# Two attention layers in one kernel: the squares of the second layer's norm are summed by full-precision products on quarters of the array, and K and V are computed by tokens

## The reference, cut to what matters

```python
def _rmsnorm(t, w):
    inv = rsqrt(mean(t * t, axis=-1, keepdims=True) + EPS)
    return t * inv * w

q = (x @ Wq.T).reshape(b, s, H, HD).transpose(0, 2, 1, 3)
k = (x @ Wk.T).reshape(b, s, HKV, HD).transpose(0, 2, 1, 3)
v = (x @ Wv.T).reshape(b, s, HKV, HD).transpose(0, 2, 1, 3)
q = _rmsnorm(q, q_norm_w)
k = _rmsnorm(k, k_norm_w)
scores = einsum('bkgqd,bksd->bkgqs', q.reshape(b, HKV, G, s, HD), k) / sqrt(HD)
attn = softmax(scores + where(rel > 0, NEG_INF, slopes * rel))
out = einsum('bkgqs,bksd->bkgqd', attn, v) ... @ Wo.T
```

## Time and profile before

| | us |
|---|---|
| median of 3 runs (1780.08 to 1784.43) | 1782.18 |
| the profiled execution | 1786.09 |
| its span, first to last instruction | 1784.4 |
| TensorE matmuls busy | 1732.1 (97%) |
| VectorE busy | 1306.6 (73%) |
| ScalarE busy | 877.3 (49%) |
| GpSimd busy | 789.8 (44%) |

### The profile page before, as it was taken

How to read it: one execution, slowest core, us unless ns; L and a number is a source line. 1 busy time by engine, 2 the same in 40 slices (tenths; PEclk the granted TensorE clock), 3 DMA queues, 4 the chain that set the end, 5 groups by cost and what they waited for, 6 DMA issues and landing times.

```text
span 1784.4 us, 28744 instructions
## 1 busy us (share of the span) xinstructions
PE 1732.1 (97%) x8864; PEld 1439.3 (81%) x8864; DVE 1306.6 (73%) x2317; ACT 877.3 (49%) x2288; POOL 789.8 (44%) x924
## 2 busy tenths in 40 slices
PE   8999999999999989997999999999999998899999
PEld 7888888888888878876788888888888887678887
DVE  5788888887888886534777777777777777755555
ACT  3656666566556553222444444444444444544543
POOL 5334435362534443344545454545454524254442
PEclk9999999999999999999999999999999999999999
DMA  4112122122222121000111010010000002022211
GB/s 148 36 66 80 61 71 94 46 91 75 65 66 81 48 73 60 1 30 1 36 30 30 29 29 29 29 29 29 29 29 29 24 0 78 18 71 59 59 59 48
DMA packets 47711, 87.77 MB, mean 49 GB/s; under 512 B 6576, under 2 KB 6576, under 8 KB 47536
## 3 DMA queue, kind: packets, MB, share of 16 engines
q1 hardware_dynamic: 47664, 87.19, 15.2%
HBM read 77.73 MB, written 9.44 MB: 49 GB/s over the span
## 4 chain that ended last, share of the span: by engine, by line
PE 56%; DVE 6%; ACT 2%; POOL 2%; issue 1%; POOLq 0%; DVEq 0%; ACTq 0%
PE ring L317 10%; PE ring L318 10%; PE ring L319 10%; PE scores L317 3%; PE scores L319 3%; PE scores L318 3%; PE turned L317 3%; PE turned L318 3%; PE turned L319 3%; PE turned L806 2%; PE scores L720 2%; PE turned L792 1%; PE turned L770 1%; PE turned L799 1%; ACT p L832 1%
## 5 line engine op out<-in xcount | busy, mean ns | idle before, releaser
L317 PE MATMUL ring<-xt_hi,w_lo 128*128 128x512 f32 x768 | 304.7, 397 | 3.9 <-DVE qt_lo L953 1.5
L318 PE MATMUL ring<-xt_lo,w_hi 128*128 128x512 f32 x768 | 303.8, 396 | 0.0
L319 PE MATMUL ring<-xt_hi,w_hi 128*128 128x512 f32 x768 | 303.7, 395 | 0.0
L317 PE MATMUL ring<-wd_hi,ot_lo 128*128 128x512 f32 x512 | 208.3, 407 | 9.4 <-DVE xt_lo L501 4.2
L823 ACT CAST pt_hi<-turned 128x512 fp32r<-128x512 f32 x192 | 100.9, 592 | 222.0 <-PE turned L799 218.8
L318 PE MATMUL ring<-wd_lo,ot_hi 128*128 128x512 f32 x512 | 202.9, 396 | 0.0
L319 PE MATMUL ring<-wd_hi,ot_hi 128*128 128x512 f32 x512 | 202.9, 396 | 0.0
L581 POOL TENSOR_SCALAR sq_hi<-sq 128x512 fp32r<-128x512 f32 x80 | 55.2, 690 | 284.5 <-ACT sq L849 266.1
L317 PEld LDWEIGHTS ring<-xt_hi,w_lo 128*128 128x128 f32 x768 | 145.1, 189 | 36.6 <-DVE qt_lo L953 2.0
L319 PEld LDWEIGHTS ring<-xt_hi,w_hi 128*128 128x128 f32 x768 | 144.8, 189 | 34.7
L318 PEld LDWEIGHTS ring<-xt_lo,w_hi 128*128 128x128 f32 x768 | 145.0, 189 | 31.5
(11 more groups left out here) (246 smaller groups left out, 4409.6 us busy)
## 6 DMA issues: line engine op xcount, KB each, us to landing
w_raw<-w_attn_dram SPq DMA_DIRECT2D x96, 256.0 KB, 2.9
wd_raw<-w_dense_dram SPq DMA_DIRECT2D x64, 256.0 KB, 2.7
code_early<-codes_dram SPq DMA_DIRECT2D x28, 256.0 KB, 2.7
absmax_early<-absmax_dram SPq DMA_DIRECT2D x56, 128.0 KB, 3.0
kept_dram<-deq_early SPq DMA_DIRECT2D x28, 256.0 KB, 2.1
stage<-kept_dram SPq DMA_DIRECT2D x28, 256.0 KB, 2.7
code_late<-codes_dram SPq DMA_DIRECT2D x14, 256.0 KB, 2.7
absmax_late<-absmax_dram SPq DMA_DIRECT2D x28, 128.0 KB, 2.9
```

The source lines that it names most:

```text
L317: nc.tensor.matmul(o, l_lo, r_hi, start=start, stop=False)
L318: nc.tensor.matmul(o, l_hi, r_lo, start=False, stop=False)
L319: return nc.tensor.matmul(o, l_hi, r_hi, start=False, stop=stop)
```

## The change

What it does, all in the second attention except for one wait:
- The K and Q squares are no longer split. `sq` has a place for each of the four heads. One step `q_rms` per half, in slots 2 and 0 between the two `out` tiles, makes four plain 32-bit products with `ones` (128 partitions x 32 columns) as the stationary operand. Head h writes to partitions 32h to 32h+31 of the side bank, so each sum is there 32 times. VectorE copies the whole bank, and `q_rms_turn` transposes full 128x128 blocks and reads one column of 32.
- K and V are computed together with tokens stationary (`kv` steps, two per half): 48 matmuls of 256 columns in place of 24 of 512. Tokens lie on partitions, so V needs no transpose, and ScalarE sums the squares of K with its accumulator. VectorE keeps K in `k_tok`, multiplies it by its root behind the Newton steps, and `k_norm` transposes it; ScalarE writes `kt_f` and `kt_hi` with the norm's weight as scale, VectorE writes `kt_lo`. GpSimd has no part in it.
- The order: slots 1 and 3 compute Q0, Q1, Q2; slots 2 and 0 compute Q3 and the two `kv` steps. The refills go in the order Q0, Q1, Q2, Q3, K, V. The lead-in and the first slot are rearranged, and the last norm's two token tiles are turned one at a time (`norm_tile`), the first on the side bank.
- SyncE waits for the loop of the second attention to end before it loads the first stages of the feed-forward, because `sq` is larger. An empty instruction stands between its wait and a weight load.

```diff
+REFILL = [[K, Q0, Q1, Q2, Q3, V], [Q0, Q1, Q2, Q3, K, V]]
 def slot_steps(b, rms):
-        tiles = [K, Q0, Q1] if b in (1, 3) else [Q2, Q3, V]
+        tiles = [Q0, Q1, Q2] if b in (1, 3) else [Q3]
...
     t = [("tile", x, half, ahead) for x in tiles]
+    t += [("kv", j, half, ahead) for j in range(2)] if rms and tiles == [Q3] else []
...
-    s += [("k_rms", half)] if rms and tiles[0] == K else []
...
-    s += [("v_turn", half)] if tiles[-1] == V else []
+    s += [("v_turn", half)] if tiles[-1] == V else [("q_rms", half)] if rms and tiles == [Q3] else []
     s += [("k_norm", 1 if b == 1 else 0)] if roots else []
-    s += [("w_next", X) for X in (Q0, Q1)] if rms and b == 3 else []
+    s += [("w_next", X) for X in (Q0, Q1, Q2)] if rms and b == 3 else []
...
-        s += [("out", 1), ("q_rms", half, 0 if tiles[0] == K else 1)]
+        s += [("out", 1)]
 def first_slot_steps(rms):
-        s = [("q_rms", 1, 0), ("tile", Q2, 1, 0)] + softmax[0] + [("w_next", K)] + softmax[1] + [("tile", Q3, 1, 0)]
-        s += [("w_next", Q0)] + softmax[2] + [("tile", V, 1, 0), ("normalise", 1), ("q_rms", 1, 1), ("w_next", Q1)]
-        return s + [("v_turn", 1)] + [("w_next", X) for X in (Q2, Q3, V)] + [("transpose",)]
+        s = softmax[0] + [("tile", Q2, 1, 0), ("w_next", Q0)] + softmax[1] + [("tile", Q3, 1, 0), ("w_next", Q1)]
+        s += softmax[2] + [("kv", 0, 1, 0), ("w_next", Q2), ("normalise", 1), ("kv", 1, 1, 0), ("q_rms", 1)]
+        return s + [("w_next", X) for X in (Q3, K, V)] + [("transpose",)]
 def lead_steps(rms):
-        s = [("norm_stats", [3]), ("tile", K, 0, 0), ("norm_root", [3], "dve"), ("norm_write", 3, "dve")]
-        s += [("tile", Q0, 0, 0), ("tile", V, 0, 0), ("k_rms", 0), ("tile", Q1, 0, 0), ("v_turn", 0)]
-        s += [("q_rms", 0, 0), ("tile", Q2, 0, 0), ("tile", Q3, 0, 0), ("norm_turn", 3), ("q_rms", 0, 1)]
-        s += [("q_rms_turn", 0), ("tile", K, 1, 0), ("roots", 0), ("tile", Q0, 1, 0), ("k_rms", 1)]
-        return s + [("tile", Q1, 1, 0), ("k_norm", 0)]
+        s = [("norm_stats", [3]), ("tile", Q0, 0, 0), ("norm_root", [3], "dve"), ("norm_write", 3, "dve")]
+        s += [("tile", Q1, 0, 0), ("tile", Q2, 0, 0), ("kv", 0, 0, 0), ("tile", Q3, 0, 0), ("norm_tile", 6, True)]
+        s += [("kv", 1, 0, 0), ("q_rms", 0), ("norm_tile", 7, False), ("q_rms_turn", 0), ("roots", 0)]
+        return s + [("tile", Q0, 1, 0), ("k_norm", 0), ("tile", Q1, 1, 0)]
# TensorE
+                    elif step[0] == "kv":
+                        _, j, half, ahead = step
+                        tile = pe_ring_bank(pe).rearrange("p (t d) -> p t d", t=2)
...
+                        for t in range(2):
+                            at = slice(half * HALF + (2 * j + t) * P, half * HALF + (2 * j + t + 1) * P)
+                            for c in range(DC):
+                                ins = mm3(tile[:, t, :], xt_hi[:, c, at], xt_lo[:, c, at], w_hi[:, K:V + 1:V - K, c, :],
+                                          w_lo[:, K:V + 1:V - K, c, :], start=c == 0, stop=c == DC - 1)
...
-                    elif step[0] == "q_rms":
-                        _, half, pair = step
...
-                        for j in range(2):
-                            h = 2 * pair + j
-                            part = (half + 1 + h) % 2
-                            row = pick[:, P - h:2 * P - h]
-                            nc.tensor.matmul(tile, row, sq_lo[:, part, :], start=j == 0, stop=False)
-                            ins = nc.tensor.matmul(tile, row, sq_hi[:, part, :], start=False, stop=j == 1)
+                    elif step[0] == "q_rms":
+                        tile = pe_ring_bank(pe, side=True)
+                        pe_sq.up(HEADS)
+                        pe.wait_ge(s_sq, pe_sq.value())
+                        for h in range(HEADS):
+                            ins = nc.tensor.matmul(tile[32 * h:32 * h + 32, :], ones[:, :], sq[:, h, :], start=True,
+                                                   stop=True)
                         pe_ring_done(ins)
# q_rms_turn, k_norm
-                            ins = nc.tensor.transpose(tile[:, q * ROWS:(q + 1) * ROWS],
-                                                      sumsq[0:ROWS, half, q * P:(q + 1) * P],
-                                                      ident[0:ROWS, 0:ROWS])
+                            ins = nc.tensor.transpose(tile[:, q * P:(q + 1) * P],
+                                                      sumsq[:, half, q * P:(q + 1) * P], ident[:, :])
-                            ins = nc.tensor.matmul(tile[:, q * P:(q + 1) * P],
-                                                   root[:, step[1], q, HEADS:ROWS].to_broadcast([P, P]),
-                                                   ident[:, :], start=True, stop=True)
+                            ins = nc.tensor.transpose(tile[:, q * P:(q + 1) * P], k_tok[:, q, :], ident[:, :])
# ScalarE
+                        for t in range(2):
+                            nc.scalar.activation(k_square[:, t, :], tile[:, t, 0, :], ACT.Square,
+                                                 accum_out=k_sum[:, 2 * j + t:2 * j + t + 1])
...
+                        act_ring_hi(nc.scalar.copy(v_hi[:, at, :], tile[:, :, 1, :]))
# VectorE, behind the Newton steps
+                        nc.vector.tensor_tensor(k_tok[:, :, :], k_tok[:, :, :],
+                                                root[:, half, :, HEADS:ROWS].to_broadcast([P, HALF // P, HD]),
+                                                ALU.mult).then_inc(s_k_scaled, 1)
# GpSimd, k_norm and the squares: gone
-                            split_steps(pool, sq_hi[:, part, :], sq_lo[:, part, :], sq[:, :], s_sq_split)
-                        split_steps(pool, kt_hi[:, cols], kt_lo[:, cols], keys, s_k_ready)
# SyncE
             if not (isinstance(sp_w.turns, int) and sp_w.n < 3):
                 sp.wait_ge(s_w, sp_w.value() - 2)
+                hold(sp)
...
+                eng.wait_ge(s_ring_full, last_slots[1])
                 for k in range(4):
                     load_stage(0, k)
```

More of the change, by code:

```diff
@@ L457, in pool_norm, with pe_norm_turn @@
                                         ALU.add).then_inc(s_shift, 1)
[L458 to L464, removed]
+            elif step[0] in ("norm_turn", "norm_tile"):
+                pool_ring.up(len(turned_tiles(step)))
+        def pe_norm_turn(pe, step):
+            for t, side in turned_tiles(step):
+                b = t // 2
+                tile = pe_ring_bank(pe, side)
                 if xn_last[0] is not None and b == BATCH - 1:
@@ L611, in attention @@
                 ffn_in["xn_last"] = p1[:, :, :].rearrange("p h k -> p (h k)").rearrange("p (t d) -> p t d", d=D)
[L612 to L615, removed]
+                k_tok = sb("k_tok", [P, HALF // P, HD], F32, scope)
+                k_sum = sb("k_sum", [P, HALF // P], F32, scope)
+                k_square = sb("k_square", [P, 2, HD], F32, scope)
                 sumsq = xn
@@ L684, in dve_lead, with pe_weights @@
                                                 as_f32(xt_hi[:, :, at]), ALU.subtract).then_inc(s_lead_lo, 1)
+            def pe_weights(pe, X, g, ahead, b):
+                if rms and b is None:
+                    pe.wait_ge(s_w, WT * (GROUPS + 1))
+                else:
+                    pe.wait_ge(s_w, WT * (GROUPS * layer + g + ahead) + REFILL[layer].index(X) + 1)
             def pe_steps(pe, steps, g, b):
@@ L959, in dve_steps @@
                             ALU.subtract))
-                    elif step[0] == "k_rms":
-                        tile = dve_ring_tile(dve, side=True)
-                        dve_ring_free(nc.vector.tensor_copy(sumsq[0:ROWS, step[1], :], tile[0:ROWS, :]))
+                    elif step[0] == "kv":
+                        _, j, half, ahead = step
+                        tile = dve_ring_tile(dve, after_hi=True).rearrange("p (t x d) -> p t x d", t=2, x=2)
+                        at = slice(2 * j, 2 * j + 2)
+                        nc.vector.tensor_scalar(ms[:, at, HEADS], k_sum[:, at], 1.0 / HD, RMS_EPS, ALU.mult, ALU.add)
+                        nc.vector.tensor_copy(k_tok[:, at, :], tile[:, :, 0, :])
+                        at = slice(4 * half + 2 * j, 4 * half + 2 * j + 2)
+                        dve_ring_free(nc.vector.tensor_tensor(v_lo[:, at, :], tile[:, :, 1, :],
+                                                              as_f32(v_hi[:, at, :]), ALU.subtract))
                     elif step[0] == "q_rms":
                         tile = dve_ring_tile(dve, side=True)
-                        rows = sumsq[0:ROWS, step[1], :]
-                        dve_ring_free(nc.vector.tensor_tensor(rows, rows, tile[0:ROWS, :], ALU.add))
+                        dve_ring_free(nc.vector.tensor_copy(sumsq[:, step[1], :], tile))
                     elif step[0] == "q_rms_turn":
@@ L1019, in pool_steps @@
                         pool_norm(pool, step)
-                    if step[0] in ("k_rms", "q_rms"):
```

(14 more changed lines are left out.)

167 lines of the change are left out of this document (79 added, 88 removed).

## The result

| | before | after |
|---|---|---|
| median, us | 1783.31 of 4 runs (1780.08 to 1784.95) | 1725.69 of 4 runs (1724.84 to 1727.61) |
| ratio, 95% interval | | 0.9681 (0.9665 to 0.9697) |
| the profiled execution, us | 1786.09 | 1727.61 |

A forecast was written before the change was run, and what follows sets the result against it. TensorE, busy 97% of 1784.4 us, was taken as the bound. Lists -13, waits -2.8, lead-in -8, first slot -6 and last slots +0.9 gave -29 to -30 us, so 1752 us, range 1740 to 1785.

The forecast's parts named there:

- the sums' price: Four full-precision products of the squares per half: five pass lengths, 2.15 us, plus shape changes, 2.3 us.
- The rival with all beside each other: All four heads' products overlap on their quarters: 0.86 instead of 2.15 us per half, 1731 us; chance 0.10.
- the 0.86 us end: Low end of the sums' cost per half, if all four products run beside each other; serial end 3.44 us.
- Turning the sums: Per half, full 128x128 transposes at 0.44 us replace four 5-row ones (0.34 us, pushing what follows by 0.10): nothing gained.
- the 0.8 of the forecast: Net saving forecast in TensorE's list of matmuls per half, -0.8 us; over 16 halves -13 us.
- The 2.8 us of the keys' sums: Keys' square product waited about 0.4 us for VectorE in six loop turns; forecast gone, -2.8 us.
- The lead-in and first slot: Stretch before the loop and its first slot: less idle TensorE and half-clock work, -8 and -6 us.
- the 2.5 us stop for `sq_lo`: TensorE's lead-in wait for GpSimd's split of the squares; forecast gone, with some 1.5 us of half-clock products after it.
- Last slots: TensorE reaches the last group's first `out` earlier against GpSimd's split of the dense weights: +0.9 us.
- About 84.7 us: Length given for one loop turn of the second attention before the change; forecast to fall to about 82.7 us.
- serial quarters: Rival: quarters go one behind the other, 3.44 instead of 2.15 us per half, 1773 us; chance 0.22.
- a falling clock: Rival: serial narrow products lower TensorE's granted clock, 1.7 us a fall; twelve falls give 1793 us; chance 0.13.

The follow-up runs named there:

- two_in_pairs: Changed kernel with heads 0 to 3 writing to quarters 0, 0, 1, 1, so two sums are overwritten and norms are wrong: 1738.9 us.
- sums_after_out: Changed kernel with `q_rms` behind `out 1`, directly ahead of the transposes, instead of ahead of it: 1727.9 us.
- changed_again: The changed kernel unedited, run once more as the others' neighbour on the same chip: 1725.4 us.
- split_back_in: Changed kernel with GpSimd splitting the squares again, into a buffer nobody reads, and `q_rms` waiting for the split: 1731.1 us.
- dense_by_head: Changed kernel, but in slot 1 the first `out` waits for each head's dense weights before that head, not for all four: 1727.1 us.
- one_quarter: Changed kernel with all four heads' sums on quarter 0, so norms are wrong but the work is the same: 1765.8 us.

## Why the prediction was right or wrong

**The step that failed** is the sums' price, and in it the sentence "the two passes of one product need the same quarter and follow each other, but the first pass of the next head needs another quarter and can start beside the second pass of the head before. Four heads then take five pass lengths". The premise holds, the order does not follow from it. I had let the first pass of head 1 wait for the second pass of head 0, as if passes started in a line; each quarter has a queue of its own (two_in_pairs), so all four heads take two pass lengths. One pass is 0.429 us, as read from the 128-column rows (0.43). 1.18 us instead of 2.3 is 1.1 us per half, 18 us over 16 halves: most of the 26 us between forecast and result. The rival with all beside each other, at 0.10, was right in its mechanism as well as in its time. I had named the 0.86 us end and argued against it with "two passes on the same quarter must queue", which is true of both and decides nothing. The rule that I cited with this term (the Trainium skill, "TensorE: Matmul & The Clock Gate", "Part 3: Packing small matmuls — row/col tiling") gives one product's duration plus a few ns for each further tile. The trace agrees to that sentence: 0.99 us for four products where two passes are 0.86, and starts 7 ns apart. The sentence beside it, that matmuls start in the program's order, is what two_in_pairs contradicts.

**The other terms of a half**, against the trace after. The ten products of the squares took 2.43 us in the trace before and not 2.33: the two of the keys' squares start 0.33 us apart where 0.23 is usual, so the squares give -1.25. V's transposes gone, -0.44 as worked out; the keys' scaling -0.45 as worked out. Turning the sums was put at no gain and gives 0.10: the 5-row transposes had also started 0.10 us late themselves, 0.33 us behind the product ahead. K and V with 24 products of 256 columns take 2.85 us a step, +0.1 as worked out. The transposes of the sums and of the keys now:
```profile
1012.74 0.60 PE L797 MATMUL turned<-ident,xn 128*128 128x128 f32 x4
1013.09 0.48 PE L323 MATMUL turned<-pt_hi,v_lo 128*128 128x512 f32 x1
...
1020.84 0.60 PE L806 MATMUL turned<-ident,k_tok 128*128 128x128 f32 x4
1021.20 0.48 PE L323 MATMUL ring<-wd_hi,ot_lo 128*128 128x512 f32 x1
```
One term was missing altogether. The twelve transposes of the probabilities ahead of the scores (lines 812 and 819 now, 799 and 806 before) take 1.30 us, here and in every slot looked at:
```profile
1024.08 0.60 PE L812 MATMUL turned<-ident,p 128*128 128x128 f32 x4
1024.51 1.04 PE L819 MATMUL turned<-ident,p 128*128 128x128 f32 x8
1025.38 0.28 PE L745 MATMUL scores<-kt_f,qt_f 128*128 128x128 f32 x1
```
Before, they took 1.43 us, from 1102.14 to the scores at 1103.57. That is 0.12 us in each slot, 0.24 per half. Single starts show where: 0.17 us from the fourth to the fifth of the eight and from there to the sixth, where 0.11 is the rule. The squares' products stood directly ahead of them in each slot and held a bank until VectorE had read the sums; with `q_rms` put there again (sums_after_out) one of these distances is 0.12 and not 0.17, so that the bank is the reason was argued, not shown. The sum: -1.25 - 0.44 - 0.10 - 0.45 + 0.10 - 0.24 = -2.4, measured -2.45. Against the 0.8 of the forecast that is 1.65 us in each of 16 halves, 26 us, about the distance between forecast and result, of which the sums' price is 18, the transposes of the probabilities 4 and the rest small.

**Waits.** The 2.8 us of the keys' sums went, as forecast. The lead-in and first slot gave back 13.8 us beside the list, where 14 was forecast. In its idle part that step was right, 10.5 us; the clock gave 5 us for 3.7, and in the same kernel's other execution (changed_again, granted 1.00 in this stretch) 1.5 us more, so the clock's part changes from execution to execution. Its reason is only partly borne out. I had read the 2.5 us stop for `sq_lo` in the earlier trace rows as GpSimd being late. split_back_in puts GpSimd's splits back, in the new order of steps, and no stop for them appears; what it adds is 2.6 us of other waits, by GpSimd holding up VectorE's small steps. How the 10.5 us of idle time divide between that, GpSimd's own lateness and the new order was not separated.

**Last slots.** +0.9 was forecast for coming earlier to the dense weights. The wait grew by 1.4 us, but the time did not: the stretch lost 2.5 us, a half's list and no more. The kernel before waited 2.0 us for VectorE in the keys' step there, and that is gone; dense_by_head shows the two waits are one, paid at either place.

**The turn.** "About 84.7 us" was a misreading: 611 us over seven turns are 87.3, and from one turning of the sums to the next it was 88.5. No term rested on it.

**Chances.** 0.84 on faster was right. 0.22 and 0.13 on serial quarters and a falling clock against 0.10 on full overlap had the weights the wrong way round: the first was excluded for this kernel by the trace, the second by one_quarter, which ran serially with the clock at 1.00.

## What to carry to other kernels

Sums over partitions that need full precision can go four at a time on quarters of TensorE's columns at the price of one product, two pass lengths plus about 0.3 us (1.18 us with both edges, where two passes are 0.86), if each quarter gets the same number of them; their order in the program does not matter. When TensorE is busy end to end, price a step by the distance from start to start, on both sides of it: single starts came 0.06 to 0.10 us late beside the steps that changed, and those in the transposes of the probabilities alone, 0.24 us per half, were a tenth of the gain. And before pricing an overlap by a chain of waits, ask for each link which resource it needs; where none is named, the link is an assumption and should be weighed as one.

## What the runs showed of the hardware that was not expected

- Passes on different quarters of the columns start independently of the program's order: a pass 14 ns behind the first, ahead of three that stand before it (two_in_pairs).
- 3.5 us of serial products with 32 of 128 columns do not lower the clock (one_quarter, granted 1.00 over 622 us).
- A VectorE step of two elements waits for the end of a GpSimd instruction that runs beside it, 1.15 us for 0.16 us of work. The kernel before shows the same: VectorE's steps at its lines 350 and 354 end at 801.12 and 803.98, GpSimd's at 801.09 and 803.96.
```profile
799.90 1.22 DVE L350 TENSOR_SCALAR rstd<-var_eps 128x2 int32<-128x2 int32 x1
...
802.82 1.16 DVE L354 SCALAR_TENSOR_TENSOR newton<-newton,var_eps 128x2 f32<-128x2 f32 x1
```
```profile
799.79 1.30 POOL L582 TENSOR_TENSOR sq_lo<-sq,sq_hi 128x512 fp32r<-128x512 f32 x1
...
802.66 1.30 POOL L582 TENSOR_TENSOR sq_lo<-sq,sq_hi 128x512 fp32r<-128x512 f32 x1
```
The Trainium skill has this in "SBUF — State Buffer", "Who interferes with whom": the two engines share a port pair as a lock, and whoever comes second stands until the other is done. The rows agree.
